# Token list from small chunks with pointer scalars, the gather's copy ahead of the experts' table, batch 0's heads turned beside the experts

## The reference

```
qk = xn @ Wqk.T + bqk   -> 8 heads, q and k of 8 numbers each (interleaved)
v  = xn @ Wv.T + bv     -> 8 heads of 8
attn = softmax(q k^T) / 8;  out = (attn v) @ Wo.T + bo
logits = xn @ W_gate + b_gate;  top_idx = top 2 of 8 experts
y = mean over those two of relu(xn @ W_e[e] + b_e[e])     (512 x 512 each)
result = x + out + y
```

## Time and profile before

| What | us |
|---|---|
| median of 3 runs | 370.81 |
| the profiled execution: time, span | 368.1, 366.4 |
| last top-2 on VectorE to gather_ready | 67.10 to 83.73 |
| first expert products | 91.07 |
| step from tile to tile, no scores / two score blocks | 3.20 / 3.66 |
| tiles 33 to 37, first products | 204.01, 208.55, 213.08, 217.62, 222.58 |
| ScalarE per expert tile: relu and high part | 0.63 + 0.58 |
| last expert products end | 229.2 |

### The profile page before, as it was taken

The page is one execution under the profiler, slowest core; times in us unless marked ns, Lnnn a source line. Parts: engine busy times, 40 slices in busy tenths (PEclk is TensorE's granted clock), DMA queues, the critical chain, the costliest instruction groups (busy, mean ns, idle before and its releaser), DMA issues.

```text
span 366.4 us, 5568 instructions
## 1 busy us (share of the span) xinstructions
PE 316.0 (86%) x1629; PEld 224.4 (61%) x1629; DVE 236.2 (64%) x555; ACT 171.6 (47%) x300; POOL 205.0 (56%) x216
## 2 busy tenths in 40 slices
PE   1488669576999999999999989299999999999955
PEld 0287659464888888888888768154546645553422
DVE  2377886792244444766768895977787978983413
ACT  0569559202233333332323224446768677586640
POOL 2096678675567766766565723858688886000000
PEclk9999887855899999999999999769999999999995
DMA  7697984503355455574434411339999999310203
GB/s 238 257 390 265 327 301 174 231 0 114 96 167 170 153 164 173 172 215 146 159 130 148 128 57 59 115 129 165 263 262 218 234 172 142 101 40 0 81 35 115
DMA packets 31003, 59.59 MB, mean 163 GB/s; under 512 B 5504, under 2 KB 5632, under 8 KB 30848
## 3 DMA queue, kind: packets, MB, share of 16 engines
q1 hardware_dynamic: 23248, 40.63, 31.2%
q0 software_dynamic: 7728, 18.62, 23.9%
HBM read 38.52 MB, written 18.61 MB: 156 GB/s over the span
## 4 chain that ended last, share of the span: by engine, by line
PE 74%; DVE 9%; DMA 6%; ACT 5%; issue 4%; SPq 2%; DVEq 0%; ACTq 0%; POOLq 0%
PE ps_s L1082 30%; PE ps_t L1014 10%; PE ps_o L1029 9%; PE ps_s L1003 7%; PE ps_t L1062 5%; PE ps_s L948 4%; DMA row_in<-in_L_attn_x_dram 3%; PE ps_m L974 3%; DMA stage<-in_L_ffn_W_e_dram 2%; ACT probs L630 2%; DVE hot_row L785 1%; PE ps_m L986 1%; PE ps_m L987 1%; PE ps_t L934 1%; DVE stats L663 1%
## 5 line engine op out<-in xcount | busy, mean ns | idle before, releaser
L1082 PE MATMUL ps_s<-w_split,t_hi 128*128 x312 | 101.4, 406 | 2.3 <-issue 1.9
L630 ACT ACTIVATE probs<-ps_t 128x512 f32<-128x512 f32 x128 | 69.6, 597 | 34.6 <-PE ps_t L1014 32.9
L811 DVE TENSOR_REDUCE row_max<-ps_s 128x1 f32<-128x512 f32 x112 | 72.2, 683 | 14.6 <-PE ps_s L1003 14.0
L476 POOL TENSOR_TENSOR row_mid<-row_mid,bias_o 128x512 f32<-128x512 f32 x39 | 50.8, 1304 | 46.7 <-ACT row_mid L574 46.7
L574 ACT ACTIVATE row_mid<-row_mid 128x512 f32<-128x512 f32 x39 | 24.7, 632 | 94.4 <-DVE row_mid L832 94.4
L1082 PEld LDWEIGHTS ps_s<-w_split,t_hi 128*128 128x128 f32 x312 | 56.4, 191 | 13.7 <-issue 3.4
L1082 PE MATMUL ps_s<-w_split,t_lo 128*128 x156 | 61.8, 396 | 0.0
L1014 PE MATMUL ps_t<-q_t,k_head 128*128 128x512 f32 x128 | 57.2, 458 | 3.1 <-ACT probs L630 2.7
L502 POOL DMA_INDIRECT acc<-expert_rows,slots_i x32 | 49.8, 1556 | 12.0 <-issue 8.5
L437 POOL TENSOR_TENSOR w_split<-stage,w_split 128x1024 fp32r<-128x1024 f32 x16 | 37.6, 2373 | 24.8 <-ACT w_split L523 24.8
L1014 PEld LDWEIGHTS ps_t<-q_t,k_head 128*128 128x128 f32 x128 | 23.9, 191 | 44.3 <-ACT probs L630 32.9
(11 more groups left out here) (132 smaller groups left out, 428.6 us busy)
## 6 DMA issues: line engine op xcount, KB each, us to landing
expert_rows<-row_mid SPq DMA_DIRECT2D x39, 256.0 KB, 2.0
stage<-in_L_ffn_W_e_dram SPq DMA_DIRECT2D x16, 512.0 KB, 6.2
row_in<-in_L_attn_x_dram SPq DMA_DIRECT2D x16, 256.0 KB, 4.4
xn_rows<-row_mid SPq DMA_DIRECT2D x16, 256.0 KB, 4.4
acc<-in_L_attn_x_dram SPq DMA_DIRECT2D x16, 256.0 KB, 9.5
out_dram<-res SPq DMA_DIRECT2D x16, 256.0 KB, 2.0
bias_e<-in_L_ffn_b_e_dram SPq DMA_DIRECT2D x1, 2048.0 KB, 7.2
k_head<-k_t SPq DMA_DIRECT2D x32, 64.0 KB, 2.8
```

Of the source, the lines that this page charges most:

```text
L476: pool.tensor_tensor(row_mid[:, n % 4, :], row_mid[:, n % 4, :], bias_o[:], ALU.add).then_inc(y_done, 1)
L630: act.activation(probs[:, n % 2, j, :], ps_t[:, j % 2, :], ACT.Exp).then_inc(exp_done, 1)
L811: dve.tensor_reduce(row_max[:, b % 2, h, i:i + 1], score_bank(n), AX.X, ALU.max).then_inc(max_done, 1)
L1082: mm = pe.matmul(ps_s[:, n % 2, :], a[:, n % 2, ks], rhs, start=(k == 0), stop=(k == 3 * KC - 1))
```

## The change

The four jobs of `FIRST` become `tile_jobs` of the experts' loop, keys behind tile K0_AT = 6, queries behind tile Q0_AT = 10. POOL clears `lay_0` behind its first six gathers, lays the keys out behind tile 1 and the queries behind tile 7. `lay_out` treats the four tiles of a batch in one instruction each, everywhere; batch 1's is all behind tile 33 and is turned at tiles 34 and 35. In the routing the casts, compares and products of two ranks become one each, `hot_tile` goes, and each chunk has its own two instructions with a per-partition operand (a pointer scalar) in place of the broadcast. The copy to `gather_i` comes ahead of the experts' table; the routing's tiles leave the first three row buffers free, and the fourth gather waits for the table.

```diff
-K_AT, Q_AT = LAY_AT + QT - 1, LAY_AT + QT
+K_AT, Q_AT = LAY_AT + 1, LAY_AT + 2
+K0_AT, Q0_AT = 6, 10
...
 def lay_out(eng, step, steps, b, which):
-            for i in tiles:
-                for at in hi_at:
-                    eng.tensor_copy(heads[:, i, :, at:at + HE].bitcast(F32R), exact[:, i]).then_inc(step, 1)
-                eng.memset(heads[:, i, :, 0:2], first).then_inc(step, 1)
-                steps[0] += 3
+            for at in hi_at:
+                eng.tensor_copy(heads[:, :, :, at:at + HE].bitcast(F32R), exact).then_inc(step, 1)
+            eng.memset(heads[:, :, :, 0:2], first).then_inc(step, 1)
+            steps[0] += 3
             eng.wait_ge(step, steps[0])
-            for i in tiles: (one subtract each)
+            eng.tensor_tensor(heads[:, :, :, lo_at:lo_at + HE], exact, heads[:, :, :, hi_at[0]:hi_at[0] + HE],
+                              ALU.subtract).then_inc(laid, 1)
...  POOL
-            link(pool.memset(lay_0[:], 0.0))
-            lay_out(pool, pool_step, steps, 0, "k")
-            for g in range(G):
-                wait_filled(pool, ("k", 0, g))
-            lay_out(pool, pool_step, steps, 0, "q")
             for n in range(RI):
+                if n == 3:
+                    pool.wait_ge(experts_known, 1)
                 gather(n)
             (half of the output bias)
+            link(pool.memset(lay_0[:], 0.0))
             for n in range(NS):
                 (add; gather n + RI)
+                if n == 1:
+                    lay_out(pool, pool_step, steps, 0, "k")
+                if n == K0_AT + 1:
+                    wait_filled(pool, ("k", 0, 1))
+                    lay_out(pool, pool_step, steps, 0, "q")
...  VectorE
-            link(dve.tensor_copy(top_f[:], top_i[:]))
+            link(dve.tensor_copy(top_f[:], top_i[:, :, 0:2].rearrange("p i r -> p r i")))
-            (two compares, two products, two token_f instructions)
+            (one of each, twice as wide; token_f with a pointer scalar)
-            link(dve.tensor_tensor(hot_tile[:], ramp..., slot_q[:, 1, :]..., ALU.is_equal))
-            for c in range(0, NC, 4):
-                dve.tensor_tensor(hot_val[:, at], hot_tile[:, c:c + 4, :], token_f[:, i:i + 4]..., ALU.mult)
-                dve.tensor_tensor(hot_row[:, at], ramp..., slot_q[:, 0, c:c + 4]..., ALU.is_equal)
+            for c in range(NC):
+                dve.tensor_scalar(hot_val[:, at[0], at[1], :], ramp[:, 0:NSE], slot_q[:, 1, c:c + 1], token_f[:, i:i + 1],
+                                  ALU.is_equal, ALU.mult).then_inc(hot_ready, 1)
+                dve.tensor_scalar(hot_row[:, at[0], at[1], :], ramp[:], slot_q[:, 0, c:c + 1], None, ALU.is_equal).then_inc(hot_ready, 1)
+            dve.wait_ge(tokens_found, 1)
+            dve.tensor_copy(gather_i[:], ps_s[:, 1, 0:NS]).then_inc(gather_ready, 1)
             (experts' table)
-            dve.wait_ge(tokens_found, 1)
-            dve.tensor_copy(gather_i[:], ps_s[:, 1, 0:NS]).then_inc(gather_ready, 1)
...  TensorE
             for c in range(NC):
-                if c % 4 == 0:
-                    pe.wait_ge(hot_ready, 2 * (c // 4 + 1))
+                pe.wait_ge(hot_ready, 2 * (c + 1))
```

More of the change, by code:

```diff
@@ L95, in attention_and_experts @@
         rout = ExitStack()
-        top_f = sb("top_f", [P, NT, 8], F32, rout)
+        sb("rows_first", [P, 3, D], F32, rout)
+        top_f = sb("top_f", [P, 2, NT], F32, rout)
         pick = sb("pick", [P, 2, NT, NE], F32, rout)
@@ L108, in attention_and_experts @@
         slot_q = sb("slot_q", [P, 2, NC], F32, rout)
-        hot_tile = sb("hot_tile", [P, NC, NSE], F32, rout)
         token_f = sb("token_f", [P, NT], F32, rout)
@@ L242, in misc_plan @@
             return [[j for j in half if 0 <= j[1] < B] for half in plan]
-        FIRST = [("k", 0, 0), ("k", 0, 1), ("q", 0, 0), ("q", 0, 1)]
         def tile_jobs(n):
-            return {MAX_AT: [("max", 0, 0)], K_AT: [("k", 1, 0), ("k", 1, 1)], Q_AT: [("q", 1, 0), ("q", 1, 1)]}.get(n, [])
+            return {K0_AT: [("k", 0, 0), ("k", 0, 1)], Q0_AT: [("q", 0, 0), ("q", 0, 1)], MAX_AT: [("max", 0, 0)], K_AT: [("k", 1, 0), ("k", 1, 1)], Q_AT: [("q", 1, 0), ("q", 1, 1)]}.get(n, [])
         def tile_scores(n):
@@ L254, in attention_and_experts @@
         LAST = [("o", B - 1, 1), ("turn", B - 1, 0)] + [("out", B - 1, i) for i in range(QT)]
-        misc = list(FIRST)
+        misc = []
         for n in range(NS):
@@ L285, in attention_and_experts, with lay_out @@
         wp_ps = ps_m[:].rearrange("p a (c n) -> p (a c) n", c=2)[:, :, 0:3 * HD]
-        def lay_out(eng, step, steps, b, which, tiles=range(QT)):
+        def lay_out(eng, step, steps, b, which):
             s, first, hi_at, lo_at, laid = ((0, 0.0, (2, 10), 18, q_laid[b]) if which == "q" else
@@ L292, in lay_out @@
             heads = lay[(Q_LAY if which == "q" else K_LAY)[b]][:].rearrange("p i (h c) -> p i h c", c=32)
-            for i in tiles:
-                for at in hi_at:
-                    eng.tensor_copy(heads[:, i, :, at:at + HE].bitcast(F32R), exact[:, i]).then_inc(step, 1)
-                eng.memset(heads[:, i, :, 0:2], first).then_inc(step, 1)
-                steps[0] += 3
+            for at in hi_at:
+                eng.tensor_copy(heads[:, :, :, at:at + HE].bitcast(F32R), exact).then_inc(step, 1)
+            eng.memset(heads[:, :, :, 0:2], first).then_inc(step, 1)
+            steps[0] += 3
             eng.wait_ge(step, steps[0])
-            for i in tiles:
-                eng.tensor_tensor(heads[:, i, :, lo_at:lo_at + HE], exact[:, i], heads[:, i, :, hi_at[0]:hi_at[0] + HE],
-                                  ALU.subtract).then_inc(laid, 1)
+            eng.tensor_tensor(heads[:, :, :, lo_at:lo_at + HE], exact, heads[:, :, :, hi_at[0]:hi_at[0] + HE],
+                              ALU.subtract).then_inc(laid, 1)
         block = ctx.enter_context(nc.Block())
@@ L603, in _ @@
             act.activation(small[:, 7, 0:1], eps_t[:], ACT.Exp).then_inc(exp_table, 1)
-            for job in FIRST:
-                keep(*job)
             for n in range(NS + 1):
@@ L734, in _ @@
             dve.wait_ge(dve_step, steps[0])
-            link(dve.tensor_copy(top_f[:], top_i[:]))
+            link(dve.tensor_copy(top_f[:], top_i[:, :, 0:2].rearrange("p i r -> p r i")))
             dve.wait_ge(consts_ready, 6)
[L737 to L741, removed]
+            link(dve.tensor_tensor(pick[:], ramp[:, 0:NE].unsqueeze(1).unsqueeze(1).to_broadcast([P, 2, NT, NE]),
+                                   top_f[:].unsqueeze(3).to_broadcast([P, 2, NT, NE]), ALU.is_equal))
             dve.memset(mask[:, NT, :], 0.0).then_inc(mask_ready, 1)
-            dve.wait_ge(dve_step, steps[0])
             dve.tensor_tensor(mask[:, 0:NT, :], pick[:, 0], pick[:, 1], ALU.add).then_inc(mask_ready, 1)
-            link(dve.tensor_scalar(token_f[:], ramp[:, 0:NT], float(P), None, ALU.mult))
-            link(dve.tensor_scalar(token_f[:], token_f[:], part[:, 0:1], None, ALU.add))
+            link(dve.tensor_scalar(token_f[:], ramp[:, 0:NT], float(P), part[:, 0:1], ALU.mult, ALU.add))
             dve.wait_ge(counted, 1)
@@ L763, in _ @@
             link(dve.tensor_tensor(place[:, 0:NT, :], ps_c[:, 0:NT, :], ecol[:, 0:1, :].to_broadcast([P, NT, NE]), ALU.add))
[L764 to L767, removed]
+            link(dve.tensor_tensor(slot_p[:], place[:, 0:NT, :].unsqueeze(1).to_broadcast([P, 2, NT, NE]), pick[:], ALU.mult))
             link(dve.tensor_reduce(slot_f[:], slot_p[:], AX.X, ALU.add))
@@ L774, in _ @@
             link(dve.tensor_copy(slot_q[:], slot_r[:].rearrange("p a r i -> p a (r i)")))
-            link(dve.tensor_tensor(hot_tile[:], ramp[:, 0:NSE].unsqueeze(1).to_broadcast([P, NC, NSE]),
-                                   slot_q[:, 1, :].unsqueeze(2).to_broadcast([P, NC, NSE]), ALU.is_equal))
-            for c in range(0, NC, 4):
-                at, i = (c // 4) % 3, c % NT
-                if c >= 12:
-                    dve.wait_ge(hot_used, c // 4 - 2)
[L783 to L786, removed]
+            for c in range(NC):
+                at, i = ((c // 4) % 3, c % 4), c % NT
+                if c >= 12 and c % 4 == 0:
+                    dve.wait_ge(hot_used, c // 4 - 2)
+                dve.tensor_scalar(hot_val[:, at[0], at[1], :], ramp[:, 0:NSE], slot_q[:, 1, c:c + 1], token_f[:, i:i + 1],
[3 more added lines that the diff above has]
+            dve.tensor_copy(gather_i[:], ps_s[:, 1, 0:NS]).then_inc(gather_ready, 1)
             link(dve.tensor_tensor(ecol[:, 3, :], ecol[:, 1, :], ecol[:, 2, :], ALU.add))
@@ L815, in lay_max @@
                 dve.wait_ge(max_done, QT * (H * b + HG * (g + 1)))
-                dve.wait_ge(q_laid[b], QT)
+                dve.wait_ge(q_laid[b], 1)
                 mx = row_max[:, b % 2, HG * g:HG * (g + 1), :].rearrange("p h i -> p i h")
@@ L841, in _ @@
                         lay_max(0, 0)
-                    if 0 <= n - LAY_AT < QT:
+                    if n == LAY_AT:
```

(13 more changed lines are left out.)

## The result

The changed kernel took 372.96 us (median of 10, 371.72 to 375.12), the kernel before beside it 369.67 (median of 10): ratio 1.0091, 95% interval 1.0064 to 1.0119, so about 3.4 us slower. The forecast was 2.2 us faster. The time lies inside the stated range, on the other side of zero: the case that came is rival 3, the pointer scalars.

The account below looks back on a forecast made before the run. VectorE's serial chain bounds the routing, TensorE the experts' tiles, late VectorE tiles 33 to 36. Terms -0.7 - 1.85 + 1.76 - 1.3 - 0.1 = -2.2 gave 365.9 profiled, 368.6 median; range 367.0 to 373.5.

Parts of the forecast that it names:

- rival 3: Token list: each pointer read costs, so the kernel is slower; 374.4 us at 0.06 a pointer, 372.4 at 0.04; chance 0.18.
- the price of a pair in the token list: A chunk's two VectorE instructions take 0.25 us with pointers free, 8.0 for 32 chunks; list gain 1.85.
- the sum of -2.2: Whole kernel: -0.7 head, -1.85 list, +1.76 transposes, -1.3 batch 1's layout, -0.1 batch 2's layout.
- the neighbour: Routing: plain 8-element tensor_scalar beside POOL, 228 ns, set against token_f's 233 to take a pointer as free.
- The rest of the list: Token list: two elements at a time, steps 0.08 shorter than durations, TensorE following at 0.21 a product, tail 0.75.
- Rival 4: Token list: each small instruction in so long a row is paid in full, 0.41 a pair, 373.7 us; chance 0.07.
- Head: Routing from the last top-2 to the token list: shorter cast 0.50, merged compares 0.1, merged products 0.1; gain 0.7.
- Copy ahead of the table: End of routing: the 1.3 us table moves beside POOL's issue and the first gather, with no wait; gain inside the list's.
- Heads: Batch 0's heads moved into the experts' tiles: 16 transposes cost TensorE 1.76; POOL's and ScalarE's work hidden.
- The clock's bound: Tile 0: TensorE's low clock might end later, each us costing half; nothing taken, bounds 0 and 1.
- Batch 1's layout: Tiles 33 to 36: one TensorE loss of 1.75 instead of 3.05; gain 1.3, bounds 0.3 and 2.
- lay_max beside POOL's memsets: Batch 2's layout, about 240 us: the 6.53 us that lay_max's tensor_scalar lies beside POOL's memsets stays.

Follow-up runs that it names:

- experiments 4: Changed kernel with constants in place of the token list's three pointer scalars a chunk, so the gather fetches row 0 only: 364.77 us in one execution.
- experiment 5: Changed kernel plus eight forms of small VectorE instructions, five of each in a row behind its last result, POOL idle: 380.17 us in one execution.
- experiment 1: Changed kernel with the old token list back (hot_tile and broadcast compares over groups of four chunks), all else as changed: 368.24 us, ratio 0.998 to the kernel before.
- experiment 3: Changed kernel with batch 0's heads back ahead of the experts on all engines, merged layout kept: 370.28 us, ratio 1.0046 to the kernel before.
- Experiment 6: Kernel before with only the merged lay_out and batch 1's layout all behind tile 33: 367.73 us, ratio 0.9938.
- Experiment 7: Kernel before with one wait added, POOL's memsets behind the last expert tile waiting until VectorE is through: 365.48 us, ratio 0.987.

## Why the prediction was wrong

- **The step that failed** is the price of a pair in the token list: "So 0.00 to 0.06 each. ... I take 0.25, by the row that shares engine, pointer and neighbour with a plain one." The pointer is 0.06, not 0 (experiments 4 and 5). Three a chunk, 32 chunks: 5.0 us between the 8.0 forecast for the pairs and the 13.0 measured, which turns the sum of -2.2 into +2.8; with 0.5 to 0.7 for tile 0's clock that is 3.3 to 3.5, and 3.4 was measured. The bound was right and the choice inside it wrong: the neighbour, 228 ns, was itself delayed by POOL, as its end 0.03 behind POOL's would have told. The undisturbed 175 ns row beside token_f's 233 gives the 0.06, and so did rival 3: "at 0.06 a pointer" 5.8 more on the forecast, found 5.0. Token_f itself was hardly delayed: 228 with POOL idle.
- **The rest of the list** was right: two elements at a time (0.14 and 0.09 start to start in experiment 5), overlap of about 0.09, TensorE able to follow. Rival 4 gives the right sign, and nearly the time, for a reason that isn't there: constants at the same size ran at 0.23 a pair (experiments 4 and 5).
- The Trainium skill (VectorE: DVE Perf Modes, the section on the fixed extra latency of SBUF-source instructions) says that many small tiles pay that latency each. The traces agree only in part: four chunks to an instruction are cheaper (0.26 a chunk with hot_tile's share, experiment 1) than one to an instruction with pointers (0.41), but not than one with constants (0.23).
- **Head**: forecast -0.7, found -0.75. The cast took 0.20 with POOL's memset gone. Of the two reasons given for its length the memset is the one: beside it the cast of 32 elements took 0.62 (experiment 3).
- **Copy ahead of the table**: the table ran beside the gather, 0.08 lost.
- **Heads**: 1.70 for the 16 transposes against 1.76; POOL's and ScalarE's part hidden as worked out, though a subtract of 256 elements took 0.81 where "at most 0.65" was forecast. The clock's bound of 0 to 1 held 0.5 to 0.7, where I had taken nothing.
- **Batch 1's layout**: -1.09 against -1.3.
- **lay_max beside POOL's memsets**: "stays", I wrote, and both compared profiles showed it. That it has two outcomes 3.1 us apart I had not seen. It is not what separates the two compared traces, which both have 6.53; which outcome the executions without a trace had is not known. Nor is it the whole spread: the kernel before has 6.53 in traces of 368.1 and 368.39, and took up to 371.22.
- The Trainium skill (SBUF — State Buffer, Who interferes with whom) says that of a two-port VectorE instruction and a GpSimd one, whichever is issued first blocks the other for its whole length. Experiment 6 agrees: 0.18 us of cast took 0.78. Experiment 7 goes further: the tensor_scalar took 1.18, 2.96 or 6.53, each time to the end of an instruction of POOL, but at 2.96 and 6.53 over several of them.

## What to carry to other kernels

An operand's kind has its own price. Ask for a row with that operand and nothing running beside it on the port it shares; a row that looks like its twin may be slow for another reason, which its end, laid beside the other engine's ends, shows. On 40 elements a per-partition scalar costs more on VectorE than running two elements at a time brings, on 128 as much, and broadcasting over several chunks is cheaper; longer instructions were not tried. When POOL has a run of memsets that nothing needs at once, make it wait for VectorE's short tensor_scalars: one wait gained 1.3%, where the whole change lost 0.9%.

## What the runs showed of the hardware

- A pointer scalar on a VectorE tensor_scalar adds 0.06 us to its duration and to the step to the next, at 40 and at 128 elements; two add 0.12. A constant second operation adds 0.00.
- A VectorE tensor_scalar of 16 elements waited 6.53 us while POOL's memsets and adds ran back to back, in another execution of the same program 2.96. The first value product came 3.1 us later with the longer one.
- VectorE instructions with two SBUF inputs are held by POOL's in the same way: the mask of experiment 6, 0.93 instead of 0.29.
